# The softmax pass of a graph layer as one flat loop over a list of (super, block) steps

## The chip, the cores and the metric

The kernel runs on one core of one Trainium2 chip. The metric is the device time of one execution in microseconds (us); lower is better. The core has five engines that run side by side, each with its own queue of instructions: TensorE (PE; its weight loads are shown as PEld), VectorE (DVE), ScalarE (ACT), GpSimd (POOL) and SyncE (SP), which here only issues transfers. They are kept in step by semaphores. In a profile "PEq", "DVEq", "SPq" are the sequencers, which handle register instructions, waits and branches ahead of the engine proper.

## What is computed

One layer of a graph network with 6250 nodes and 200000 edges; the edges are sorted by the node they point to (dst). Two convolutions over the edges come first, then attention over each node's incoming edges:

```python
logits = (q[dst] * k[src]).sum(-1) * scale + (edge_attr @ ew + eb)
amax = jax.ops.segment_max(logits, dst, num_segments=n)
pe = jnp.exp(logits - amax[dst])
ssum = jax.ops.segment_sum(pe, dst, num_segments=n)
w = pe / jnp.clip(ssum[dst], 1e-06)
o = jax.ops.segment_sum(w[:, :, None] * v[src], dst, num_segments=n)
```

The change lies in the last part of it: the exponentials of the logits below their node's maximum, and the sums over each node of pe and of pe times v.

## The kernel before

The edges are cut into 392 supers of 512 edges (4 tiles of 128). The nodes are cut into 49 blocks of 128. As dst is sorted, a super touches one block, at times two or three. A word for each super in `ranges` holds its first and end block; it is read on the chip by each engine that needs it (`span`, L587: a TENSOR_LOAD and register instructions that cut the word, L597). The profile counts 440 additions at L1618, one of which is a dummy at the start, so there are 439 (super, block) pairs.

The program is a row of phases with a barrier between them: tables, conv1, node update, tables, conv2, node update, tables, `logits_pass` (logits of every edge, and maxima of windows of nodes), `node_maxima` (turns those maxima through DRAM into `max_parts`, three bf16 parts of each node's maximum), `softmax_pass`, and the last node update. The change touches `node_maxima` and `softmax_pass`.

`softmax_pass` runs a loop over supers, four slots in a turn (`slots`), and every engine has a fixed place in it. In a slot the stages belong to different supers, the lag being given by MAXIMUM, BELOW, LOAD_V, EXPONENT, WEIGHT, SCATTER = 1, 2, 2, 3, 4, 5. Inside a slot the stages that work per block run an inner loop (`pairs`) whose ends are registers:

- SP loads the 512 dst numbers of a super, spread over 128 partitions (`sm_dst`, L1508, float32), and its v rows (`sm_v`, L1513).
- ACT makes the one-hot `sm_pick` [node, edge] for each pair in two activations (L651 and L655), and the exponential (L1589).
- PE picks each edge's maximum out of `max_parts` for each pair (L684: 4 matmuls of 24 columns), between an opening and a closing matmul (L1569, L1573).
- DVE adds the three parts of the maximum (L1646), subtracts (L1648), makes the other one-hot `sm_hot` [edge, node] (L1629), and adds a pair's sums to `acc` (L1618).
- POOL multiplies v with the exponentials (L1525).
- PE sums a pair into PSUM (L1554, the scatter: 4 float32 matmuls of 136 columns, each two instructions in the trace), and then runs two matmuls of 512 columns whose result is used nowhere (FILL, L1563).

Semaphores order it: the scatter waits for `vals`, `hot` and `sums_free`, `sm_hot` for the scatter of the slot before, and SP's loads for `picked` and `vals`.

## Time and profile before

| | us |
|---|---|
| median of 3 runs | 8706.32 |
| lowest, highest | 8701.71, 8711.42 |
| the profiled execution | 8703.69 |
| its span | 8701.6 |
| mean granted TensorE clock | 0.822 of full |
| softmax pass in it, from 7201.2 to 8575.3 | 1374.1 |

The span is the time between the first and last instruction of the profiled execution; some 2 us lie around it. The phases follow one another, so a phase that becomes shorter by x us makes the execution shorter by x us, and what matters is the spacing of the pairs inside the softmax pass and the length of `node_maxima` ahead of it.

### The profile page before, as it was taken

The numbers are of one execution on the slowest core, as the hardware profiler recorded it, in microseconds if no ns is written. First come the engines' busy times: TensorE is split into PE (matmuls) and PEld (weight loads), VectorE is DVE, ScalarE is ACT, GpSimd is POOL, SyncE is SP. The second block draws the span as 40 slices with busy tenths as digits, with TensorE's granted clock in tenths as the row PEclk, the third lists the DMA queues.
The fourth block names the chain that finished last, engine by engine and source line by source line (L and its number), as shares of the span: only waits on it lengthen the run. The fifth ranks groups of instructions, "written<-read, shape, count | busy, mean of one in ns | idle before, by whom it ended". The sixth has DMA issues, their size and how long they took to land. (4 is left out here: it accounts for less than half of the span.)

```text
span 8701.6 us, 251909 instructions
## 1 busy us (share of the span) xinstructions
PE 6115.6 (70%) x44185; PEld 3967.9 (46%) x44285; DVE 5542.8 (64%) x14457; ACT 4053.9 (47%) x6964; POOL 5050.9 (58%) x5122
## 2 busy tenths in 40 slices
PE   1688888888648888888884566666655556777774
PEld 1455555555435555555553333333333324555553
DVE  4666677777666666776775566666666664444445
ACT  2445555555344555555552344444444445555552
POOL 0677777777437777777770676666655543332221
PEclk9899999999879999999996555555555559999996
DMA  4455555555225555555551666666655545554442
GB/s 144 125 135 134 134 135 134 134 136 134 66 73 134 134 134 134 134 133 133 133 131 37 173 177 173 175 173 169 159 149 145 137 110 161 161 154 148 142 138 74
DMA packets 1002317, 1182.73 MB, mean 136 GB/s; under 512 B 305441, under 2 KB 697612, under 8 KB 1000786
## 3 DMA queue, kind: packets, MB, share of 16 engines
q1 hardware_dynamic: 776470, 668.01, 27.8%
q0 software_dynamic: 225792, 514.10, 22.5%
q8 instruction: 20, 0.33, 0.0%
q14 instruction: 35, 0.29, 0.0%
HBM read 1039.63 MB, written 141.89 MB: 136 GB/s over the span
## 5 line engine op out<-in xcount | busy, mean ns | idle before, releaser
L844 POOL DMA_INDIRECT conv_rows<-src_table,conv_idx x3136 | 3114.3, 993 | 955.2 <-issue 912.9
L1265 POOL DMA_INDIRECT lg_rows<-kv_table,lg_idx x1568 | 1485.7, 948 | 958.5 <-issue 496.0
L764 PEld LDWEIGHTS ps<-conv_vals,conv_hot 128*128 128x128 f32 x7024 | 916.2, 191 | 506.2 <-issue 349.0
L1327 ACT ACTIVATE acc<-ps,neg_win 128x512 f32<-128x512 f32 x976 | 634.5, 687 | 952.7 <-DVE lg_top L1413 902.3
L947 DVE TENSOR_REDUCE conv_var<-conv_sq 128x32 f32<-128x512 f32 x784 | 536.4, 684 | 764.2 <-ACT conv_sq L908 740.6
L868 PE MATMUL ps<-conv_rows,ident_b 128*128 128x512 bf16 x2352 | 645.9, 384 | 526.9 <-DMA conv_rows<-src_table,conv_idx 480.4
L764 PE MATMUL ps<-conv_vals,conv_hot 128*128 128x129 f32 x7024 | 938.2, 276 | 109.0 <-DVE acc L750 109.0
L908 ACT ACTIVATE conv_sq<-ps 128x512 f32<-128x512 f32 x784 | 468.1, 597 | 1113.0 <-PE ps L874 997.4
L1525 POOL TENSOR_TENSOR sm_vals<-sm_v,sm_vals 128x512 f32<-128x512 f32 x392 | 414.8, 1058 | 952.9 <-ACT sm_vals L1589 952.9
L729 DVE TENSOR_TENSOR conv_hot<-conv_node_row,dst_cols 128x512 f32 (+1 forms) x878 | 604.8, 689 | 388.6 <-PE ps L764 304.3
L655 ACT ACTIVATE conv_pick<-conv_apart,one_col 128x512 f32 x878 | 633.7, 722 | 456.2 <-PE ps L684 289.2
L1554 PE MATMUL ps<-sm_vals,sm_hot 128*128 128x136 f32 x3512 | 567.8, 308 | 368.2 <-DVE acc L1618 163.0
L889 PE MATMUL ps<-conv_y,ident 128*128 128x512 f32 x1568 | 807.2, 596 | 3.5 <-DVE conv_y L977 3.5
L684 PE MATMUL ps<-dst_parts,conv_pick 128*128 x10536 | 771.0, 222 | 8.3 <-issue 4.2
L1413 DVE CUSTOM_DVE_ANT_0 acc<-ps,acc 128x512 f32<-128x512 f32 x976 | 635.4, 688 | 144.6 <-DVE tops L1368 125.1
L1288 PE MATMUL ps<-w_bias,lg_ea 39*128 39x8 bf16 x1568 | 96.0, 164 | 885.6 <-DVE logits L1394 885.6
L1554 PEld LDWEIGHTS ps<-sm_vals,sm_hot 128*128 128x128 f32 x3512 | 476.0, 204 | 423.9 <-DVE acc L1618 247.5
L684 PEld LDWEIGHTS ps<-dst_parts,lg_pick 128*128 x5268 | 524.3, 140 | 307.2 <-issue 303.9
L684 PEld LDWEIGHTS ps<-dst_parts,conv_pick 128*128 x10536 | 610.6, 99 | 116.0 <-issue 25.2
L913 ACT ACTIVATE conv_vals<-ps 128x512 f32<-128x512 f32 x784 | 468.1, 597 | 408.6 <-PE ps L889 408.5
L651 ACT ACTIVATE conv_apart<-conv_dst,neg_node 128x512 f32<-128x512 f32 x878 | 628.0, 715 | 40.1 <-DMA conv_dst<-dst_rows 20.0
L684 PE MATMUL ps<-dst_parts,lg_pick 128*128 x5268 | 634.4, 308 | 6.0 <-DVE lg_pick L669 4.9
(230 smaller groups left out, 9954.6 us busy)
## 6 DMA issues: line engine op xcount, KB each, us to landing
conv_dst<-dst_rows SPq DMA_DIRECT2D x784, 256.0 KB
v_edges<-lg_rows SPq DMA_DIRECT2D x392, 256.0 KB
sm_dst<-dst_rows SPq DMA_DIRECT2D x392, 256.0 KB, 3.3
sm_v<-v_edges SPq DMA_DIRECT2D x392, 256.0 KB, 2.7
conv_rows<-src_table,conv_idx POOLq DMA_INDIRECT x3136
lg_dst<-dst_half SPq DMA_DIRECT2D x392, 128.0 KB
conv_ea<-ea_parts SPq DMA_DIRECT2D x784, 36.0 KB
lg_rows<-kv_table,lg_idx POOLq DMA_INDIRECT x1568
```

The lines of the kernel that those rows point to most:

```text
L651: act.activation(apart, dst, ACT.Square, bias=neg_node[:, bass.ds(blk, 1)]).then_inc(picks.apart_made, 1)
L655: act.activation(picks.buffer(act, turn), apart, ACT.Relu, bias=one_col[:, 0:1], scale=-1.0).then_inc(picks.made, 1)
L684: last = pe.matmul(to[:, j, :], names, part, start=False, stop=False, skip_group_check=True)
L729: dve.tensor_tensor(hot[:, :, :], node_row[:, bass.ds(blk, 1), :].to_broadcast([P, TILES, P]), dst_cols[:, bass.ds(TILES * s, TILES)].unsq ...
L764: last = pe.matmul(bank(SUMS[g])[:, 0:self.width], self.hot[g][:, j, :], vals[:, j, 0:self.width], start=(j == 0), stop=(j == TILES - 1))
L844: pool.indirect_dma_start(rows[r][:, j, :], None, src_table, bass.IndirectOffsetOnAxis(idx[r][:, j:j + 1], 0)).then_inc(S["rows_in"][r], 16)
L868: last = pe.matmul(bank(MSG[r]).rearrange("p (j c) -> p j c", c=D), ident_b[:, :], rows[r][:, :, p * D:(p + 1) * D], start=(p == 0), stop= ...
L889: pe.matmul(bank(SHIFT[r % 2]).rearrange("p (j c) -> p j c", c=D), ident[:, :], y[r % 2][:, :, :], start=False, stop=True, skip_group_chec ...
L1265: pool.indirect_dma_start(rows[r][:, j, :], None, kv_table, bass.IndirectOffsetOnAxis(idx[r][:, j:j + 1], 0)).then_inc(S["rows_in"][r], 16)
L1327: act.activation(far[h], bank(AGAIN[r % 2]), ACT.Square, bias=neg_win[:, bass.ds(w + h, 1)], scale=PEN).then_inc(S["far"], 1)
L1413: dve.tensor_tensor_reduce(masked[h], bank(SPREAD_TO[r % 2]), far[h], 1.0, NEG, ALU.subtract, ALU.max, top[:, h:h + 1]).then_inc(S["top"], 1)
L1554: last = pe.matmul(bank(SUMS[r % 2])[:, 0:ACC_W], hot[r % 2][:, j, :], vals[r][:, j, :], start=(j == 0), stop=(j == TILES - 1))
```

## The change

`node_maxima` now also makes a list of steps. DVE takes the two block numbers of each super, makes running sums of the pair counts (9 additions over 392 numbers), PE spreads two rows over all partitions, and a loop over columns of 256 steps each finds super and block of every step. The codes are turned by PE, packed two to a word (15 bits each), written to `steps_d` in DRAM and read back into one partition of the memory that held `dst_parts`. The number of turns is `(pairs + 9) >> 2`, here (439 + 9) >> 2 = 112, so that the loop runs over 448 steps; those past the end name a spare block, number 49, that nothing reads. The maxima are stored negated.

`softmax_pass` is one loop over these steps, with no inner loop. Each of SP, PE and DVE reads one word for two steps and cuts super and block from it. The stages are:

- SP: dst (now from `dst_half`, int16, half the bytes) and v for every step, in that order, each with a wait of its own.
- DVE: the one-hot pick (L1759: compare 512 int16 numbers with the node number), `sm_hot` (L1751), and the addition (L1742). L1646 and L1648 are gone.
- PE: the scatter as before (L1686), and BELOW: one matmul of 32 columns (L1699), 16 matmuls of 8 columns (L1703: for each tile a large constant and the three negated parts), and the logits through the identity in float32 (L1706). Edges that don't belong to the step's block end at -2^64, so that their exponential is 0. The FILL matmuls and L1560 are gone.
- ACT: the exponential alone, read from PSUM (L1717).
- POOL: as before (L1667).

```diff
+STEP_BITS, SUPER_BITS = 15, 9
+STEP_COLS = 76
+STEP_WORDS = STEP_COLS * P
...
-        dst_parts = sb("dst_parts", [P, BLOCKS, 3, D], BF16)
-        acc = sb("acc", [P, BLOCKS, ACC_W])
+        dst_raw = sb("dst_raw", [P, 2 * STEP_WORDS], BF16)
+        dst_parts = dst_raw[:, 0:BLOCKS * 3 * D].rearrange("p (b k c) -> p b k c", k=3, c=D)
+        steps, turns, columns = dst_raw[0:1, :].bitcast(I32), sb("turns", [1, 1], I32), sb("columns", [1, 1], I32)
+        acc = sb("acc", [P, BLOCKS + 1, ACC_W])
...
+                        pe.wait_ge(summed, 1)
+                        pe.matmul(bank(1)[:, 0:SUPERS], ones[:, :], sums[:, TOTALS, BEHIND:BEHIND + SUPERS], start=True, stop=True)
+                        pe.matmul(bank(2)[:, 0:SUPERS + 1], ones[:, :], gaps[:, :], start=True, stop=True).then_inc(spread, 1)
+                        pe.wait_ge(coded, 1)
+                        for h in range(2):
+                            last = pe.transpose(bank(3)[0:STEP_COLS, h * P:(h + 1) * P], block_of[:, :, h], ident[:, :])
+                        last.then_inc(turned, 1)
...
+                        sp.wait_ge(packed, 1)
+                        sp.dma_start(steps_d.rearrange("(c p) -> c p", p=P), codes[:, 0, :]).then_inc(stored, 16)
+                        sp.wait_ge(stored, 16)
+                        sp.dma_start(steps, steps_d.rearrange("(a n) -> a n", a=1)).then_inc(stored, 16)
+                        sp.wait_ge(stored, 32)
...
+                        while reach < SUPERS:
+                            done(dve.tensor_tensor(sums[:, 1 - now, BEHIND:], sums[:, now, BEHIND:],
+                                                   sums[:, now, BEHIND - reach:BEHIND - reach + SUPERS], ALU.add))
+                            reach, now = 2 * reach, 1 - now
...
+                        done(dve.tensor_scalar(turns[:, :], turns[:, :], 9, None, ALU.add))
+                        done(dve.tensor_scalar(turns[:, :], turns[:, :], 2, None, ALU.arith_shift_right))
...
+                        with dve.Fori(0, last_column) as c:
+                            done = chain(dve, walk, base + COLUMN_STEPS * c)
+                            for h in range(2):
+                                at = lambda x: x[:, bass.ds(c, 1), h]
+                                done(dve.tensor_scalar(under[:, :], bank(1)[:, 0:SUPERS], at(step_f), None, ALU.is_le))
+                                done(dve.tensor_reduce(at(super_of), under[:, :], AX.X, ALU.add))
+                                done(dve.tensor_tensor(under[:, :], under[:, :], gaps_of[:, 0:SUPERS], ALU.mult))
+                                done(dve.tensor_reduce(skipped[:, :], under[:, :], AX.X, ALU.add))
+                                done(dve.tensor_tensor(at(block_of), at(block_of), skipped[:, :], ALU.add))
...
+                PICK, BELOW, HOT, EXPONENT, WEIGHT, SCATTER, ADD = 1, 2, 2, 3, 4, 5, 6
+                LEAD = 3
...
+                    for i in range(LEAD):
+                        turn(i)
+                    with eng.Fori(LEAD, end) as i:
+                        turn(i)
...
+                            t, r, k = stage(0)
+                            if r % 2 == 0:
+                                load_word(sp, "sp", words[r // 2], 2 * k + r // 2)
+                            own = sp.snap(super_at(sp, words, r))
+                            row = dst_half[bass.ds(own, 1), :].to_broadcast([P, SUPER])
+                            rows = v_edges[bass.ds(own, 1), :, :].rearrange("a p (j c) -> (a p) j c", c=D)
+                            hold(sp, made["pick"], t - (DEPTH - 1), made["sp_paced"])
+                            sp.dma_start(dst[r][:, :], row).then_inc(dst_in[r], 16)
+                            hold(sp, made["vals"], t - (DEPTH - 1), made["sp_paced"])
+                            sp.dma_start(v[r][:, :, :], rows).then_inc(v_in[r], 16)
...
-                                for _ in range(FILL):
-                                    pe.matmul(bank(SPARE), ident_b[:, :], constant[:, :], start=True, stop=True)
...
+                                t, r, k = stage(SCATTER)
+                                pe.wait_ge(made["vals"], t + 1)
+                                pe.wait_ge(made["hot"], t + 1)
+                                wait(pe, made["added"], t - 1)
+                                for j in range(TILES):
+                                    last = pe.matmul(bank(SUMS[r % 2])[:, 0:ACC_W], hot[r][:, j, :], vals[r][:, j, :],
+                                                     start=(j == 0), stop=(j == TILES - 1))
+                                last.then_inc(made["sums"], 1)
+                            if stage(BELOW):
+                                t, r, k = stage(BELOW)
+                                if r % 2 == 0:
+                                    load_word(pe, "pe", words[r // 2], 2 * k + r // 2)
+                                blk, own = block_at(pe, words, r), super_at(pe, words, r)
+                                top = max_parts[:, bass.ds(blk, 1), :, :].rearrange("p a k c -> p (a k) c")
+                                own = logits[:, bass.ds(own, 1), :].rearrange("p a c -> p (a c)")
+                                to = bank(BELOW_AT[r % 2])[:, 0:TILES * HEADS]
+                                wait(pe, made["weight"], t - 1)
+                                pe.matmul(to, digit_w[:, :], far_row[:, :], start=True, stop=False, skip_group_check=True)
+                                pe.wait_ge(made["pick"], t + 1)
+                                for j in range(TILES):
+                                    for part in [far_cols[:, :]] + [top[:, p, :] for p in range(3)]:
+                                        pe.matmul(to[:, j * HEADS:(j + 1) * HEADS], pick[r % 2][:, j * P:(j + 1) * P], part,
+                                                  start=False, stop=False, skip_group_check=True)
+                                pe.matmul(to, ident[:, :], own, start=False, stop=True, skip_group_check=True).then_inc(made["below"], 1)
...
+                                act.wait_ge(made["below"], t + 1)
+                                wait(act, made["sums"], t - (DEPTH - 1))
+                                act.activation(vals[r][:, :, D:ACC_W], bank(BELOW_AT[r % 2])[:, 0:TILES * HEADS].rearrange("p (j h) -> p j h", h=HEADS),
+                                               ACT.Exp).then_inc(made["weight"], 1)
...
+                            if stage(ADD):
+                                t, r, k = stage(ADD)
+                                to = acc[:, bass.ds(dve.snap(added_to[r], min_val=0, max_val=BLOCKS), 1), :].rearrange("p a c -> p (a c)")
+                                dve.wait_ge(made["sums"], t + 1)
+                                wait(dve, made["added"], t)
+                                dve.tensor_tensor(to, bank(SUMS[r % 2])[:, 0:ACC_W], to, ALU.add).then_inc(made["added"], 1)
+                            if stage(HOT):
+                                t, r, k = stage(HOT)
+                                blk = block_at(dve, words, r)
+                                dve.reg_mov(added_to[r], blk)
+                                own = dst_cols[:, bass.ds(TILES * super_at(dve, words, r), TILES)].unsqueeze(2).to_broadcast([P, TILES, P])
+                                start = first[:, bass.ds(blk, 1)]
+                                if not isinstance(t, int) or t >= DEPTH:
+                                    hold(dve, made["sums"], t - (DEPTH - 1), made["dve_paced"])
+                                dve.scalar_tensor_tensor(hot[r][:, :, :], own, start, lanes, ALU.subtract, ALU.is_equal).then_inc(made["hot"], 1)
+                            if stage(PICK):
+                                t, r, k = stage(PICK)
+                                if r % 2 == 0:
+                                    load_word(dve, "dve", words[r // 2], 2 * k + r // 2)
+                                nodes = node_of[:, bass.ds(block_at(dve, words, r), 1)]
+                                wait(dve, made["below"], t - 1)
+                                hold(dve, dst_in[r], 16 * (k + 1), made["dve_paced"])
+                                dve.tensor_scalar(pick[r % 2][:, :], dst[r][:, :], nodes, None, ALU.is_equal).then_inc(made["pick"], 1)
```

Two places show what stands in a row on an engine. The first is DVE in the loop of the pass, one slot of before with one pair. Names are tiles; ISA and REGISTER_ALU are register instructions of the sequencer.

```order
L1629 SCALAR_TENSOR_TENSOR sm_hot<-dst_cols,sm_first,ps 128x512
L615 ISA
L1618 ISA
L1618 TENSOR_TENSOR acc<-ps,acc 128x136
L1496 ISA
L605 COMPARE_AND_BRANCH
L587 ISA
L587 TENSOR_LOAD ranges
L597 REGISTER_ALU
L597 ISA
L597 REGISTER_ALU
L1640 ISA
```

After these come one more register instruction, L1646 and L1648. Now one step on the same engine:

```order
L1742 ISA
L1742 TENSOR_TENSOR acc<-ps,acc 128x136
L1625 ISA
L1746 REGISTER_ALU
L1746 ISA
L1751 REGISTER_ALU x2
L1751 ISA
L1751 SCALAR_TENSOR_TENSOR sm_hot<-dst_cols,sm_first,ps 128x512
L1621 TENSOR_LOAD dst_raw
L1621 ISA
L1759 REGISTER_ALU x2
L1759 ISA
```

The branches of the inner loop and the reduction with its dependent subtraction are gone, and the pick L1759 stands at the end of the step; the load of a word comes in every second step. The second place is PE. Before, behind the scatter of a slot:

```order
L1554 MATMUL ps<-sm_vals,sm_hot 128x136 x4
L1496 ISA
L605 COMPARE_AND_BRANCH
L1560 MATMUL ps<-ident_b 128x1
L1563 MATMUL ps<-sm_constant,ident_b 128x512 x2
L1569 MATMUL ps<-sm_zeros,digit_w 128x96
L605 UNCONDITIONAL_BRANCH
L605 ISA
L684 ISA
L684 MATMUL ps<-max_parts,sm_pick 128x24
```

Now:

```order
L1686 MATMUL ps<-sm_vals,sm_hot 128x136 x4
L1625 ISA
L1699 MATMUL ps<-sm_far_row,digit_w 128x32
L1703 MATMUL ps<-sm_far_cols,sm_pick 128x8
L1703 REGISTER_ALU x2
L1703 ISA
L1703 MATMUL ps<-max_parts,sm_pick 128x8
L1703 ISA
L1703 MATMUL ps<-max_parts,sm_pick 128x8
L1703 ISA
L1703 MATMUL ps<-max_parts,sm_pick 128x8
L1703 MATMUL ps<-sm_far_cols,sm_pick 128x8
```

The two wide matmuls and the branches went; 16 narrow ones came, of which the first three parts each need a register instruction of their own. In the loop of four steps the order of the changed program has, beside data instructions, 45 register and branch instructions and 2 loads on PE, 51 and 2 on DVE, 21 and 2 on SP; before it had on DVE 61 and 4 for four slots with one pair each.

## Rows read from the trace of the kernel before

**Rows 1.** by stretch: busy us (count) of five engines, PEclk, DMA share, GB/s

```profile
5000.00:6000.00 1000.00, 663.33 (x4336) 371.08 (x4334) 662.91 (x2010) 426.93 (x908) 688.08 (x727) 0.51 0.65 174
...
7202.00:7219.00 17.00, 7.68 (x36) 5.04 (x37) 11.19 (x17) 11.20 (x18) 3.74 (x4) 0.50 0.77 233
...
7400.00:8000.00 600.00, 427.93 (x3170) 302.71 (x3215) 276.97 (x742) 321.32 (x566) 187.35 (x178) 0.95 0.52 156
```

**Rows 2.** groups of the pass: count, busy us, mean ns, idle before and releasers

```profile
L1554 PE MATMUL ps<-sm_vals,sm_hot 128*128 128x136 f32 x3477 | 562.7, 309 | 366.2 <-DVE acc L1618 161.0 <-issue 114.9 <-POOL sm_vals L1525 89.4
...
L1525 POOL TENSOR_TENSOR sm_vals<-sm_v,sm_vals 128x512 f32<-128x512 f32 x390 | 412.7, 1058 | 947.3 <-ACT sm_vals L1589 947.3
L1629 DVE SCALAR_TENSOR_TENSOR sm_hot<-dst_cols,sm_first,ps 128x512 f32<-128x512 f32 x435 | 324.5, 746 | 279.6 <-PE ps L1554 183.4 <-issue 95.9
...
L1563 PE MATMUL ps<-sm_constant,ident_b 128*128 128x512 bf16 x676 | 225.9, 405 | 10.0 <-issue 3.6
```

**Rows 3.** timeline of DVE inside the pass: start, length, instruction, idle before

```profile
7753.68 0.75 DVE L1629 SCALAR_TENSOR_TENSOR sm_hot<-dst_cols,sm_first,ps 128x512 f32<-128x512 f32 x1 [2.45 <-PE ps L1554]
7754.34 0.29 DVE L1618 TENSOR_TENSOR acc<-ps,acc  x1
7755.51 0.26 DVE L1646 TENSOR_REDUCE sm_highest<-ps 128x32 f32<-128x96 f32 x1 [0.88 <-issue]
...
7756.50 0.75 DVE L1629 SCALAR_TENSOR_TENSOR sm_hot<-dst_cols,sm_first,ps 128x512 f32<-128x512 f32 x1 [0.38 <-issue]
...
7759.17 0.75 DVE L1629 SCALAR_TENSOR_TENSOR sm_hot<-dst_cols,sm_first,ps 128x512 f32<-128x512 f32 x1 [0.39 <-issue]
```

**Rows 4.** timeline of PE and its weight loads (PEld) near the pass's end

```profile
8507.71 2.17 PE L1554 MATMUL ps<-sm_vals,sm_hot 128*128 128x136 f32 x8 [0.36 <-POOL sm_vals L1525]
...
8518.40 0.17 PEld L684 LDWEIGHTS ps<-max_parts,sm_pick 128*128 x4
...
8518.76 0.47 PEld L684 LDWEIGHTS ps<-max_parts,sm_pick 128*128 x4 [0.20 <-issue]
...
8526.61 1.19 PE L1554 MATMUL ps<-sm_vals,sm_hot 128*128 128x136 f32 x8 [0.67 <-issue]
```

**Rows 5.** timeline of SP's queue (SPq): two transfers issued one behind the other

```profile
7763.40 0.33 SPq L1513 DMA_DIRECT2D sm_v<-v_edges  x1
...
7764.00 0.33 SPq L1508 DMA_DIRECT2D sm_dst<-dst_rows  x1
```

**Rows 6.** the page's DMA issues: KB each, median us from issue to landing

```profile
sm_dst<-dst_rows SPq DMA_DIRECT2D x392, 256.0 KB, 3.3
```

**Rows 7.** SP's own waits in the pass: us in total, times, longest

```profile
SPq L83 <- POOL sm_vals L1525: 568.4, 342, 5.3
```

**Rows 8.** single lines: shortest, median and longest ns

```profile
L587 DVEq TENSOR_LOAD <-ranges x342: 300/305/326, 7302.2 to 8497.0; - x171
...
L669 DVE TENSOR_SCALAR lg_pick<-lg_dst,node_of x439: 352/353/594, 4818.1 to 7151.0; 128x512 int16 x147
```

**Rows 9.** timeline: POOL's multiply and DVE's subtraction beside it, and one without

```profile
7212.52 1.06 POOL L1525 TENSOR_TENSOR sm_vals<-sm_v,sm_vals 128x512 f32<-128x512 f32 x1 [11.09 <-ACT sm_vals L1589]
...
7213.02 0.60 DVE L1648 TENSOR_TENSOR sm_below<-logits,sm_highest 128x32 f32<-128x32 f32 x1
...
7755.93 0.19 DVE L1648 TENSOR_TENSOR sm_below<-logits,sm_highest 128x32 f32<-128x32 f32 x1 [0.17 <-DVE sm_highest L1646]
```

**Rows 10.** timeline where the maxima end and the pass begins, and its last instruction

```profile
7189.47 0.33 SPq L1441 DMA_DIRECT2D max_nodes<-by_window  x1
...
7197.36 0.56 DVE L1455 CAST max_parts<-max_by_block 128x392 bf16<-128x392 f32 x1 [7.92 <-DMA max_by_block<-max_nodes]
...
7201.22 1.30 SPq L1508 DMA_DIRECT2D sm_dst<-dst_rows  x3
...
7205.06 5.61 DVE L1609 MEMSET acc<- 128x6664 f32 x1 [1.34 <-issue]
...
8575.03 0.30 DVE L1618 TENSOR_TENSOR acc<-ps,acc  x1 [1.55 <-PE ps L1554]
```

More of the change, by code:

```diff
@@ L1488, in enter @@
[L1488 to L1500 removed]
+                dst, v = deep("dst", [P, SUPER], I16), deep("v", [P, TILES, D])
```

263 lines of the change are left out of this document (131 added, 132 removed).

## The prediction

> **What bounds the kernel now.** I read the table by stretch first. The logits pass holds PE at half clock, 0.51, with PE busy 0.66; the softmax pass runs at 0.95 with PE busy 0.71, DVE 0.46, ACT 0.54, POOL 0.31 [rows 1]. No engine is full, so the spacing of the pairs must come from hand-overs and from sequencers. The groups say so: PE's scatter stood idle 366 us in the pass and `sm_hot` on DVE 280 us, mostly for each other [rows 2]. Then the seam: the pass lasts from SP's first load at 7201.22 to the end of the last addition at 8575.33, 1374.1 us [rows 10]. That is 1374.1 / 439 = 3.13 us for a pair.
>
> The timeline of DVE shows of what a pair is made. Three `sm_hot` start at 7753.68, 7756.50 and 7759.17, 2.82 and 2.67 us apart, and the last two stood idle before for "issue" alone [rows 3]. DVE's data instructions fill some 1.5 us of that. The rest is its sequencer: from the addition (7754.34) to L1646 (7755.51) are 1.17 us, in which stand one load of a word, 0.305 us [rows 8], and some ten other things (8 register or branch instructions, a wait, the dispatch). (1.17 - 0.305) / 10 = 0.087, so I take **0.09 us for a small sequencer instruction on DVE**, an estimate. Test on before: 61 / 4 = 15.3 small ones a slot, 3 waits and 4 dispatches make 22.3 x 0.09 = 2.0, plus the load 0.31, plus 0.42 for the subtraction that must wait for the end of L1646 (7755.93 - 7755.51) [rows 3, 9]: 2.7 us. The rows have 2.67 to 2.82, the mean 3.13. So before is bound by DVE's sequencer, and runs 1.15 above its own count through waits on PE.
>
> **The change part by part.** I cost one step on each engine, as all are in order and a step passes through each.
>
> DVE: 51 / 4 = 12.8 small instructions, 2 waits, 3 dispatches: 17.8 x 0.09 = 1.60, plus half a load 0.15: 1.75 us. Its data work is 0.75 + 0.29 + the pick; the same form (512 int16 numbers against a node number) took 0.353 in the logits pass [rows 3, 8]. Sum 1.39, hidden under the sequencer. L1646, L1648 and the dependent 0.42 are gone.
>
> PE: a register instruction with the narrow matmul behind it costs 0.12: four such weight loads took 0.47 where the sequencer made the pace ((0.47 - 0.10) / 3), and 0.17 where they were queued, 0.025 apart [rows 4]. 45 / 4 = 11.3 small, 2 waits: 13.3 x 0.12 = 1.60. The 14 matmuls without a register instruction between them at 0.025 are 0.35, half a load 0.15: 2.1 us; with 0.10 for a small one 1.8. I take 2.0. PE's own work at full clock is the scatter 1.19, 17 short ones x 0.025 = 0.43, two float32 loads for the identity at 1.19 / 8 = 0.15 each: 1.9, partly under the sequencer. The FILL matmuls that go (226 us busy in the records [rows 2]) ran in PE's gaps and free nothing by themselves.
>
> SP: two transfers at 0.60 from issue to issue [rows 5], half a load, 3 more small: 1.65 us. dst now stands behind v in the queue, and v waits for POOL four steps back; SP already waits 568 us so [rows 7]. From vals(n-5) to vals(n) that loop costs 0.6 + 0.35 to issue, 3.3 to land [rows 6], 0.35 pick, about 1.7 on PE and ACT, 1.06 POOL: 7.4 us for 5 steps, 1.5 a step. Hidden below 2.0. POOL needs 1.06 plus a hand-over, ACT less.
>
> So **the slowest queue needs 2.0 us** where before needed 2.7. The waits now reach 3 to 6 steps back (four `hot`, four `vals`) and no stage waits for the same step on the engine it just served; I add 0.25 for what is left, less than the 0.4 of before: T = 2.25.
>
> A small matmul costs PE 0.025 when queued [rows 4]. The Trainium skill, "TensorE: Matmul & The Clock Gate", Part 1, has that floor too, but adds that with decoding in microcode each takes about 62 ns. By the page 16 would be 1.0 us in place of 0.4 and PE some 2.6 a step; the rows speak for the smaller number.
>
> Number of steps: 448 (9 more than pairs), 9 x 2.25 = 20 us of empty work, counted in. Start of the pass: before, `acc`'s memset ran from 3.8 to 9.5 us into the pass [rows 10]; now it stands ahead of DVE's first pick, 8.5 us. The last step's scatter and addition come 3 us late. **Pass after = 11.5 + 448 T** = 11.5 + 1008 = 1019.5 us, against 1374.1.
>
> The list: no row shows it, so I build it from an instruction over 392 numbers, 0.56 [rows 10], 0.60 with its wait. Ahead of the loop 14 of these and two longer ones, 10.7; 11 short ones at 0.25 and two others, 3.9; the loop runs (439 + 264) >> 8 = 2 times with 8 long and 2 short and some 10 register waits: 13; the end 2.7. Then two transfers: up to 2.4 and 4 us, as near those of the maxima, where from issue at 7189.47 to the cast at 7197.36 two in a row took 7.9 [rows 10]. Sum 36.7, starting at 7189.5 as the copy does: 7226.2, with 1.4 for the barrier 7227.6. Before the pass began at 7201.2, so **+26; I take +28**, with the wait for PE's spread. Bounds: +20 (long ones partly cheaper) and +45 (every short one at 0.6). The old wait for the maxima, their casts and three instructions for the sign lie beside it.
>
> Sum: -1374.1 + 1019.5 + 28 = -326.6. Profiled execution 8703.7 - 326.6 = 8377.1; the median of before is 2.6 above it: **8380 us**.
>
> **The rivals.** In general the time is 8706.3 - 1374.1 + 28 + 11.5 + 448 T = 7371.7 + 448 T; without any saving 448 T would be 1334.6.
>
> 1. *DVE's pick and POOL's multiply shut each other out.* While POOL multiplied from 7212.52 to 7213.58, the subtraction on DVE ended at 7213.62 and took 0.60; elsewhere 0.19 [rows 9]. If the pick does the same, DVE's data work grows from 1.39 by up to 1.06 to 2.45, and with some wait T = 2.65: 7371.7 + 1187.2 = **8559**. For: both recur each step, and the step's order can lock them. Against: POOL is free half of the time. The Trainium skill, "SBUF — State Buffer", "Who interferes with whom", says that such a one-input compare in a two-port mode and a GpSimd instruction exclude one another for a whole instruction; it is this rival's rule.
>
> 2. *The clock stays at half.* PE enters the pass at half clock (0.50 from 7202 to 7219) [rows 1], and FILL, which kept it working between scatters, is gone. At half the scatter takes 2.17 [rows 4]; two identity loads at 2.17 / 8 are 0.54, the narrow ones 0.4, hand-over 0.2: T = 3.3, and PE is the bound: 7371.7 + 1478.4 = **8850, slower**. It decides against the change where T passes 1334.6 / 448 = 2.98. For: the logits pass stays at 0.51 though PE is busy 0.66 of it, much of that in short or low-row matmuls. Against: at T = 3.3 PE would be busy nearly always and over half of it with the full float32 scatter, denser than in the first 17 us of the pass now (7.68 of 17 us), after which the clock rose to 0.95. The same page on the clock gate holds that half clock is the default and activity lifts it.
>
> 3. *The waits vanish altogether.* T = 1.9: **8223**.
>
> 4. *Depth doesn't help*: engines stay in lock step through waits that sit in sequencers, T about 2.95: 8693.
>
> **How the numbers follow.** T from 2.05 to 2.45 (8290 to 8469): 0.50. Rival 1, up to 2.85: 0.22. Rival 3: 0.12, of which I leave out a third, below 1.92. Rival 2: 0.12. Rival 4: 0.04. Leaving out the last two and 0.04 at the fast end gives 8230 to 8650 with 0.80 in it; the list's bounds (-8, +17) lie inside. A measurement of this kernel can tell some 0.2%, 17 us, from no change. Faster: 0.50 + 0.22 + 0.12 + 0.02 = 0.86; same 0.02; slower 0.12.
>
> **What the profile would show.** The pass at about 1020 us with its hots 2.25 apart; PE's clock at 0.95 or more and PE busy over 0.8; picks at 0.35 if POOL doesn't hold them, up to 1.4 if it does; SP waiting less for POOL; some 28 us more between the two passes. Wrong would be: PEclk near 0.5 (rival 2), picks of 1 us (rival 1), DVE or PE idle on each other for 0.8 us a step (rival 4), or a list of over 45 us.

## Time and profile of the changed kernel: the result

| | median, us | runs | granted clock, mean |
|---|---|---|---|
| kernel before | 8704.15 | 4 (8701.71 to 8711.42) | |
| changed kernel | 8761.89 | 4 (8752.45 to 8765.83) | 0.751 |

The ratio is 1.0063, with a 95% interval from 1.0046 to 1.0081: the change makes the kernel 0.6% slower, where 8380 us were forecast and 8230 to 8650 was the range. The profiled execution spans 8750.2 us.

The page by forty slices (of some 219 us each, digits in tenths) says what happened. The softmax pass fills the 34th to the 39th slice and part of the two beside them:

```profile
PE   1688888888557888888884666666655549999995
...
PEclk9899999999779999999996555555555555555555
```

PE is full from there to the end of the pass, and its clock never leaves 5 tenths. In the kernel before the same stages ran at 0.95 with PE busy 0.71 [rows 1]. The table by stretch of the changed kernel (busy us and count for PE, PEld, DVE, ACT and POOL, then PEclk, DMA share, GB/s):

```profile
7215.00:7230.00 15.00, 6.65 (x70) 5.67 (x70) 11.99 (x11) 1.05 (x4) 3.17 (x3) 0.50 0.50 147
7230.00:7600.00 370.00, 369.92 (x3184) 333.50 (x3184) 238.38 (x354) 23.29 (x118) 124.59 (x118) 0.50 0.43 126
...
8000.00:8590.00 590.00, 589.85 (x5072) 531.23 (x5072) 378.90 (x564) 37.10 (x188) 197.99 (x188) 0.50 0.44 125
```

In 590 us PE is idle for 0.15 us. 188 multiplies of POOL in 590 us are 3.14 us a step. The groups of the pass, 7230 to 8600 (count, busy us, mean ns, idle before and its releaser), answer to [rows 2]:

```profile
L1686 PE MATMUL ps<-sm_vals,sm_hot 128*128 128x136 f32 x3486 | 943.3, 452 | 0.3
...
L1667 POOL TENSOR_TENSOR sm_vals<-sm_v,sm_vals 128x512 f32<-128x512 f32 x436 | 460.6, 1056 | 910.3 <-ACT sm_vals L1717 910.3
L1759 DVE TENSOR_SCALAR sm_pick<-sm_dst,node_of 128x512 bf16<-128x512 int16 x436 | 427.1, 980 | 69.3 <-issue 67.3
...
L1742 DVE TENSOR_TENSOR acc<-ps,acc 128x136 f32 x436 | 130.7, 300 | 258.7 <-PE ps L1686 258.7
...
L1717 ACT ACTIVATE sm_vals<-ps 128x32 f32<-128x32 f32 x436 | 86.0, 197 | 1284.9 <-PE ps L1706 1284.9
```

The scatter's matmul has a mean of 452 ns where before had 309, and stands idle 0.3 us in the whole pass where before had 366. So the waits that the change was to take away are indeed gone; every other engine now waits for PE. The pick on DVE takes 980 ns in the mean; [rows 8] has 353 for its form.

One step, in the timeline of the changed kernel (start, length, instruction, idle before):

```profile
8000.89 2.16 PE L1686 MATMUL ps<-sm_vals,sm_hot 128*128 128x136 f32 x8
...
8001.55 1.06 POOL L1667 TENSOR_TENSOR sm_vals<-sm_v,sm_vals 128x512 f32<-128x512 f32 x1 [2.21 <-ACT sm_vals L1717]
8001.87 0.89 DVE L1759 TENSOR_SCALAR sm_pick<-sm_dst,node_of 128x512 bf16<-128x512 int16 x1 [0.32 <-issue]
...
8002.98 0.20 PE L1699 MATMUL ps<-sm_far_row,digit_w 2*128 2x32 bf16 x1
8003.29 0.30 DVE L1742 TENSOR_TENSOR acc<-ps,acc 128x136 f32 x1 [0.54 <-PE ps L1686]
8003.56 0.61 PE L1706 MATMUL ps<-logits,ident 128*128 x2
...
8004.19 2.18 PE L1686 MATMUL ps<-sm_vals,sm_hot 128*128 128x136 f32 x8
```

PE's step is the scatter, 2.09 us to the next instruction; then the constant row and 16 narrow matmuls, 0.58 (8002.98 to 8003.56); then the identity with two float32 loads, 0.43 in three steps of four and 0.57 to 0.63 in the fourth, which is the one shown. The pick began at 8001.87, under POOL's multiply of 8001.55 to 8002.61, and ended at 8002.76, just behind it.

From SP's first `sm_dst` at 7215.03 to its last, 447 steps later, are 1398.8 us: **T = 3.13 us**, the measure by which the passes are compared below.

The seam, where the list of steps is made (answering to [rows 10]; the four transposes of the maxima stand at 7175.8 here and at 7187.5 in before):

```profile
7192.56 0.63 DVE L1541 TENSOR_SCALAR max_under<-ps,max_step_f 128x392 f32<-128x392 f32 x1 [0.61 <-DVE max_block_of L1532]
...
7204.71 0.24 DVE L1547 TENSOR_SCALAR max_super_of<-max_super_of 128x152 f32<-128x152 f32 x1 [0.21 <-DVE max_block_of L1545]
...
7207.47 0.25 SPq L1482 DMA_DIRECT2D steps_d<-max_codes  x1
...
7209.64 0.21 SPq L1484 DMA_DIRECT2D dst_raw<-steps_d  x1
...
7215.03 0.37 SPq L1650 DMA_DIRECT2D sm_dst<-dst_half  x1
```

From the transposes to the first load of the pass are 39.2 us (7215.03 - 7175.8); before, 13.7 (7201.22 - 7187.5). The list costs 25.5 us. The stages ahead of it ended 11.7 us earlier in this execution than in that of before, and the change doesn't touch those.

### The profile page after: what moved, and what is told of

Same layout as the page of the kernel before. It is cut to its first block and busy times, and to the rows that moved or that the text cites. A ratio compares the mean times of both kernels' runs of the same rounds, so it can differ in the third digit from the quotient of the medians.

```text
span 8750.2 us, 252225 instructions
## 1 busy us (share of the span) xinstructions
PE 6531.3 (75%) x49078; PEld 4528.4 (52%) x49079; DVE 5834.3 (67%) x14184; ACT 3416.9 (39%) x6139; POOL 5099.3 (58%) x5175
## 5 line engine op out<-in xcount | busy, mean ns | idle before, releaser
L1667 POOL TENSOR_TENSOR sm_vals<-sm_v,sm_vals 128x512 f32<-128x512 f32 x444 | 469.1, 1056 | 932.8 <-ACT sm_vals L1717 932.8
L1686 PE MATMUL ps<-sm_vals,sm_hot 128*128 128x136 f32 x3544 | 958.9, 452 | 0.3
L1686 PEld LDWEIGHTS ps<-sm_vals,sm_hot 128*128 128x128 f32 x3544 | 839.9, 335 | 11.5
L693 PE MATMUL ps<-dst_raw,conv_pick 128*128 x10536 | 766.1, 221 | 8.4 <-issue 3.9
L693 PEld LDWEIGHTS ps<-dst_raw,lg_pick 128*128 x5268 | 525.7, 142 | 309.2 <-issue 306.1
L693 PEld LDWEIGHTS ps<-dst_raw,conv_pick 128*128 x10536 | 606.8, 98 | 115.2 <-issue 24.4
L693 PE MATMUL ps<-dst_raw,lg_pick 128*128 x5268 | 635.7, 311 | 5.6 <-DVE lg_pick L678 4.8
```

The source lines that it names most:

```text
L693: last = pe.matmul(to[:, j, :], names, part, start=False, stop=False, skip_group_check=True)
L1686: last = pe.matmul(bank(SUMS[r % 2])[:, 0:ACC_W], hot[r][:, j, :], vals[r][:, j, :], start=(j == 0), stop=(j == TILES - 1))
```

## The experiments

Theory A: the change lost the full clock because it took FILL out. Theory B: something else in the new pass holds it down. Once that was settled, two questions followed: what bounds the pass at full clock (P: PE; V: DVE, with its pick held up by POOL), and whether the clock depends on how the pass is entered.

### FILL put back, and taken from the kernel before

```diff
 last.then_inc(made["sums"], 1)
+for _ in range(2):
+    pe.matmul(bank(5)[:, :], ident_b[:, :], constant[:, 0:512], start=True, stop=True)
```

> The changed kernel, with the two 128x512 bf16 FILL matmuls of the kernel before put back behind each step's scatter (they write a bank that nobody reads). Theory A: the change lost the full clock because it took FILL out; with FILL the pass goes back to 0.95 or more. PE then needs 1.19 for the scatter, 0.10 + 0.42 + 0.30 for the difference and 2 x 0.213 for FILL, 2.44 us a step in place of 3.14: 8762 + 448 x (2.44 - 3.14) = 8448 us, up to 8542 if VectorE's pick and GpSimd's multiply together set 2.65. Theory B: something else in the new pass holds the clock down, its fullness for one (PE busy 1.00 of the pass). The granted clock stays 0.50 and FILL costs 2 x 0.427 a step: 8762 + 448 x 0.85 = 9145 us.

Measured: 8440.58 us (8436.33 to 8446.00), ratio to before 0.9696 [0.9683, 0.9710]. Its pass:

```profile
7230.00:7260.00 30.00, 23.91 (x203) 18.48 (x203) 20.11 (x24) 1.38 (x7) 7.40 (x7) 0.51 0.46 138
7260.00:7300.00 40.00, 39.19 (x484) 30.81 (x483) 33.30 (x50) 3.35 (x17) 17.97 (x17) 1.00 0.58 160
7300.00:7600.00 300.00, 292.00 (x3625) 230.16 (x3622) 253.78 (x375) 24.64 (x125) 132.10 (x125) 1.00 0.58 164
```

The clock is at 1.00 from 7260 on and a step takes 2.42 us, 0.71 less than without 1024 columns of work that nobody needs. Theory A holds; theory B's 9145 is ruled out, since PE is busy 0.97 of the time here as well.

With one FILL matmul in place of two (`range(1)`):

> As the run with two FILL matmuls a step, but with one. Theory A, and one is enough to keep the full clock: PE 2.23 us a step, VectorE's sequencer (1.75 to 2.0) and the waits near it: 8762 + 448 x (2.25 - 3.14) = 8363 us, or near 8500 if VectorE's pick and GpSimd's multiply set 2.5. Theory A, and one is not enough: clock 0.50, T = 3.14 + 0.43 = 3.57, 8953 us. Theory B: 8953 us too, so this run tells A from B only together with the one of two.

Measured: 8953.34 us (8950.60 to 8958.80), ratio 1.0286 [1.0271, 1.0300]; the pass from 7300 to 8800:

```profile
7300.00:8800.00 1500.00, 1499.48 (x11736) 1203.55 (x11735) 902.95 (x1259) 82.62 (x419) 442.90 (x420) 0.50 0.39 110
```

The clock stayed at half, and T is 3.56: the matmul added its 0.43 to a full queue.

FILL only behind the first seven scatters, six each time:

```diff
+for _ in range(6 if isinstance(t, int) else 0):
+    pe.matmul(bank(5)[:, :], ident_b[:, :], constant[:, 0:512], start=True, stop=True)
```

> The changed kernel with six FILL matmuls behind each of the first seven scatters alone, none in the loop. Theory A1 (the clock has two stable states here: what is too thin at half clock, 3.14 us a step, is dense enough at full clock, where a step is shorter): the clock rises in the first 30 us of the pass and stays up, T near 2.2, 8762 + 20 - 448 x 0.94 = 8360 us. Theory A2 (the new loop cannot hold the full clock however it enters): the clock rises for a stretch and falls back to 0.50, 8765 to 8785 us. Theory B: never rises, 8782 us.

Measured: 8762.74 us (8750.13 to 8764.89), ratio 1.0063 [1.0049, 1.0077], theory A2. The last of these FILL matmuls starts at 7266.9, and the stretches around it are:

```profile
7248.00:7252.00 4.00, 4.00 (x52) 2.71 (x51) 2.05 (x3) 0.20 (x1) 1.06 (x1) 1.00 0.26 97
...
7272.00:7276.00 4.00, 3.95 (x56) 3.52 (x55) 2.97 (x6) 0.39 (x2) 2.11 (x2) 1.00 0.70 183
7276.00:7280.00 4.00, 3.70 (x35) 3.45 (x35) 2.81 (x6) 0.39 (x2) 2.11 (x2) 0.80 0.65 199
7280.00:7284.00 4.00, 4.00 (x47) 3.52 (x46) 2.44 (x5) 0.20 (x1) 1.06 (x1) 0.50 0.54 157
```

The clock was up before 7248 and was lost again some 11 us after the last FILL had started, in the stretch in which PE has 0.3 us without work. Lifted in this way, the new loop by itself doesn't hold it.

The kernel before without FILL:

```diff
-                FILL = 2
+                FILL = 0
```

> The kernel before with FILL = 0, nothing else. It prices that one part of the change by itself. Theory A: the pass falls to clock 0.50. Each of the 439 pairs then has 2.17 for the scatter, about 0.6 for the maximum and subtraction, and the waits between VectorE and TensorE that the old order has: T about 3.9 in place of 3.13, 8706 + 439 x 0.8 = 9057 us (bounds 8900 to 9150). Theory B, by which FILL has nothing to do with the clock: 8690 to 8706 us at 0.95.

Measured: 8756.61 us (8754.86 to 8763.76), ratio 1.0061 [1.0046, 1.0075]. The mechanism was right, the price was not:

```profile
7230.00:8600.00 1370.00, 1157.54 (x6239) 955.59 (x6237) 641.53 (x1609) 700.49 (x1229) 400.32 (x379) 0.50 0.49 145
```

The pass runs at half clock, but the old order has room: the scatter, which stood idle 366 us in the pass [rows 2], takes the longer matmuls partly into its gaps and now stands idle 210:

```profile
L1554 PE MATMUL ps<-sm_vals,sm_hot 128*128 128x136 f32 x3401 | 925.5, 453 | 210.0 <-DVE acc L1618 143.4 <-issue 42.9 <-POOL sm_vals L1525 13.7
```

The pass grows by 51 us, not by 350. The four together:

| | FILL 2 x 512 | no FILL |
|---|---|---|
| order of before | 8704 (0.95 in the pass) | 8757 (0.50) |
| new order, with its list | 8441 (1.00) | 8762 (0.50) |

Reordering with FILL in place is worth 263 us (some of it can be the clock, which rose from 0.95 to 1.00), and nothing at half clock; FILL is worth 53 us in the old order and 321 in the new one. The change made both steps at once, and each price was worked out as if the other stood still.

### What bounds the pass at full clock

The next twelve kernels ran on three other chips, four on each, on which the stages ahead of the pass take longer: the kernel before takes 11,406 us beside the first four kernels, 11,290 and 11,409 beside the others, and in the run with FILL of 2 x 384 the transposes before the list stand at 9912.7 where e1_fill2 has 7187.8. The pass itself takes what it took on the first chip where the same kernel ran on both (T = 2.21 for FILL 2 x 256 with the clock lifted, below), so it is compared by T.

GpSimd multiplies one tile of four (the values of the other three are zero):

> The changed kernel with two FILL matmuls a step, and GpSimd multiplies only the first of the four tiles of a step (the values of the other three are left at zero, so their part of the sum is missing from the result). The multiply goes from 1.06 to some 0.3 us. With FILL a step takes 2.40 us, in which VectorE's pick takes 1.06 in place of 0.35. Theory V (the pick and the multiply exclude each other, and VectorE's 0.75 + 0.29 + 1.06 with its issue sets the 2.40): the picks fall below 0.5 and T falls to TensorE's own load, about 2.3: 8441 - 448 x 0.1 = 8396 us. Theory P (TensorE's queue sets it: 0.97 busy, the rest its word loads): the picks fall as well, but T stays: 8435 to 8445 us. Theory N (no exclusion; the pick is slow by itself in this pass): the picks stay at 1.0.

Measured: 11,141.1 us; T = 2.42, no different from e1_fill2. All the picks of this run (shortest, median and longest ns):

```profile
L1765 DVE TENSOR_SCALAR sm_pick<-sm_dst,node_of x447: 346/431/519, 9951.2 to 11025.7; 128x512 bf16<-128x512 int16 x149
```

In e1_fill2 the median is 1085 ns. So GpSimd's multiply does lengthen the pick, by 0.65 us, and it costs nothing: theory P.

FILL of 384 columns in place of 512:

> The changed kernel with two FILL matmuls a step of 384 columns in place of 512. At full clock that takes 2 x 0.053 = 0.11 off TensorE's 2.40 to 2.44 us a step. Theory P (TensorE sets T): 8441 - 448 x 0.11 = 8392 us. Theory V (VectorE sets T): 8441 us. If the full clock does not hold with so little work: 0.50 and T = 3.14 + 2 x 0.32 = 3.78, 9048 us.

Measured: 11,103.7 us, T = 2.30 (1028.2 / 447), clock 1.00: 0.12 us a step, where P had 0.11 and V nothing. Its pass on PE alone, where one turn of the loop (four steps) ends:

```profile
10502.35 1.17 PE L1687 MATMUL ps<-sm_vals,sm_hot 128*128 128x136 f32 x8
...
10504.53 1.17 PE L1687 MATMUL ps<-sm_vals,sm_hot 128*128 128x136 f32 x8
...
10507.13 1.19 PE L1687 MATMUL ps<-sm_vals,sm_hot 128*128 128x136 f32 x8 [0.25 <-issue]
```

Three steps of four take 2.18 to 2.19 us, and PE's instructions follow each other without a gap; the fourth takes 2.60.

The pick made by ScalarE, in two instructions:

```diff
-dve.tensor_scalar(pick[r % 2][:, :], dst[r][:, :], nodes, None, ALU.is_equal)
+act.activation(apart[r % 2][:, :], dst[r][:, :], ACT.Square, bias=neg_nodes)
+act.activation(pick[r % 2][:, :], apart[r % 2][:, :], ACT.Relu, bias=one_col, scale=-1.0)
```

> The changed kernel with two FILL matmuls a step, and ScalarE makes the one-hot of the nodes (Square of the difference, then Relu of one minus it, 0.72 us each as in the kernel before) in place of VectorE. ScalarE then has 1.44 + 0.20 and its sequencer, some 2.1 us a step, VectorE only 1.04 and its sequencer. Theory P: T stays 2.40, 8441 us. Theory V: T falls to TensorE's load, 2.3, 8396 us. ScalarE as a new bound (in-order exponent behind two activations): T up to 2.6, 8530 us.

Measured: 11,138.3 us, T = 2.42: P again.

The pick as a two-input instruction of VectorE (`scalar_tensor_tensor(pick, dst, nodes, ones, is_equal, mult)`):

> The changed kernel with two FILL matmuls a step, and VectorE makes the pick with a two-input instruction (compared with the node number, times a tile of ones), which computes the same. Theory V: a two-input instruction does not exclude GpSimd's multiply; it takes 0.55 to 0.75 us in every step in place of 1.06, and T falls by 0.1, 8396 us. Theory P: the duration falls, T stays at 2.40, 8441 us. Theory N: it is no shorter than 1.06.

Measured: 11,148.5 us, T = 2.41. The expectation of 0.55 to 0.75 us was wrong; the group from 10100 to 10900:

```profile
L1763 DVE SCALAR_TENSOR_TENSOR sm_pick<-sm_dst,node_of,sm_constant 128x512 bf16<-128x512 int16 x334 | 473.5, 1418 | 37.7 <-issue 35.9
```

It takes 1.42 us, and T is what it was. The first two picks of the pass, made before POOL's first multiply, took 0.75 and 0.74 us and the third, under it, 1.50; so this form is held up as well. VectorE had just room for it: it is busy 754.75 of the 800 us.

TensorE's load of a word of the list moved from behind FILL into the scatter, with FILL 2 x 384:

```diff
 for j in range(TILES):
     last = pe.matmul(...)
+    if j == 1 and stage(BELOW)[1] % 2 == 0:
+        word_of(stage(BELOW))
```

> The changed kernel with two FILL matmuls of 384 columns, and TensorE's load of a word of the list stands between the second and third matmul of the scatter in place of behind FILL. With FILL of 384 columns a step takes 2.30 us, of which TensorE stands idle for issue 0.32 + 0.25 us in two steps, behind the load. Theory P (TensorE's queue sets T): the load is covered by matmuls already queued, T = 2.30 - 0.2 = 2.1, 90 us off the pass (1028 to 940). Theory V (VectorE, whose pick is held to the end of GpSimd's multiply, is near its bound with 0.88 of its time busy): T stays at 2.2 to 2.3, 0 to 40 us. The clock stays at 1.00 in both.

Measured: 10,984.2 us beside 11,289.6, T = 2.33. No gain, rather 0.03 lost: a turn still has its step of 2.60, and one of the other three now takes 2.31 in place of 2.19. My reading of the gaps was wrong: they don't stand behind a load of a word (two in a turn) but once in a turn of the loop. With ScalarE's pick on top of it:

> As the run with the word's load in the scatter and FILL of 384 columns, and ScalarE makes the pick in two instructions of 0.72 us. It tells whether VectorE's pick holds that run. Theory V: with the pick gone from VectorE, T falls below that run's, to 2.1. Theory P: no faster than that run. If ScalarE (1.64 us busy a step and its own load and registers) becomes the bound, slower than that run: T 2.3 to 2.4.

Measured: 10,996.0 us, T = 2.33. VectorE was not what held it.

A prefetch hint for the branch at the end of TensorE's loop (`hint_back_edge`), with FILL 2 x 384, and beside it the same kernel without the hint:

> The changed kernel with two FILL matmuls of 384 columns and a branch prefetch hint at the top of TensorE's loop. With 2 x 384, three steps of four take 2.18 us and the one that closes the loop's iteration 2.63: a gap of 0.4 before the scatter. If the gap is the loop's branch fetching its instructions, the hint takes it away: T = 2.19, 112 x 0.4 = 45 us less, some 8345 us where the kernel with 2 x 384 has 8390. If VectorE, whose own loop closes as well, holds it: no change. If it is the load of the word: no change.

> The kernel with two FILL matmuls of 384 columns again, beside the other runs on one chip, and to see whether its clock rises in every run. By the spacing in its first profile 52 us less than with 512 columns: 8390 us where the kernel before has 8704.

Measured: 11,122.6 us with the hint (T = 2.34), 11,126.4 without (T = 2.31). The hint takes nothing away; the gap before the scatter at a turn's end is `[0.38 <-issue]` with it, where e6_fill2x384 has 0.25, so it costs some 0.1 us a turn. What the 0.4 us are stays open: that they come once in a turn is shown, that it is the branch is not. The clock was at 1.00 from some 35 us into the pass to its end in both profiles, and no run of either stood apart.

### How the pass is entered

FILL 2 x 320:

> The changed kernel with two FILL matmuls of 320 columns, load of the word where the changed kernel has it. 2 x 384 columns a step held the full clock, one of 512 did not. If 2 x 320 hold it: T = 2.30 - 0.053 = 2.25, 24 us less in the pass than with 384, 1004 us. If not: clock 0.50 for at least part of the pass, T = 3.14 + 0.53 = 3.67 there, up to 1640 us for the pass.

Measured: one run at 10,972.9 us, three from 11,140.8 to 11,193.8. The profile shows why:

```profile
9850.00:10300.00 450.00, 449.83 (x3556) 369.34 (x3555) 263.12 (x368) 24.12 (x122) 129.05 (x122) 0.50 0.36 107
10320.00:11000.00 680.00, 660.66 (x8809) 558.95 (x8807) 570.14 (x911) 59.92 (x303) 320.84 (x304) 1.00 0.65 176
```

The same loop ran at half clock for over 450 us, 3.69 us a step (122 in 450), then at full clock to its end, 2.24 us a step (304 in 680). Both are what its work amounts to at that level. A run at 3.69 us a step from start to end would take near 11,600 us, an estimate from 2 x 256, below, with 11,539 at 3.55. So by their times the clock rose in mid-pass in the other two of these three runs too, and near the start in the run of 10,972.9. Nothing in the program changes at 10,300; what made the clock rise there is open.

FILL 2 x 256, with the word's load moved:

> As the run with the word's load in the scatter, with two FILL matmuls of 256 columns. As many columns as the one of 512, which left the clock at 0.50; but the steps are some 0.2 us shorter at full clock. If the clock goes by work in a stretch of time once it is up but must first rise at half clock, it stays at 0.50: T = 3.57, pass about 1590 us. If the way it is cut or the shorter step lifts it: T near 2.0 to 2.2, 900 to 980 us.

Measured: 11,539.3 us, ratio 1.0222, clock 0.50 throughout, T = 3.55. The moved load alone doesn't keep the clock down: in e9_early_384, with 2 x 384, it was up 25 us into the pass. That asked for the opposite test, to lift the clock first and then give less:

```diff
+lead = isinstance(t, int)
+for _ in range(6 if lead else 2):
+    cols = SUPER if lead else 256
+    pe.matmul(bank(5)[:, 0:cols], ident_b[:, :], constant[:, 0:cols], start=True, stop=True)
```

> The changed kernel with six FILL matmuls of 512 columns behind each of the first seven scatters (they lifted the clock to 1.00 from 7246 on when they stood alone) and two of 256 columns in the loop. In the loop alone 2 x 256 left the clock at 0.50 through the whole pass. Two states with memory (what holds the full clock is less than what brings it): the clock stays at 1.00, T = 2.30 - 2 x 0.053 = 2.19, pass about 1000 us with the slow start. No memory: it falls back within some 20 us of the loop's start as it did without FILL, T = 3.57, pass about 1590 us.

Measured: 11,056.2 us beside 11,409.3, ratio 0.9694 [0.9680, 0.9709], T = 2.21:

```profile
9900.00:9950.00 50.00, 36.11 (x400) 27.61 (x404) 33.32 (x48) 3.92 (x15) 13.91 (x14) 0.79 0.42 128
...
10300.00:10600.00 300.00, 290.96 (x3973) 252.31 (x3972) 248.44 (x411) 27.00 (x137) 144.82 (x137) 1.00 0.65 179
```

The loop that stayed at half clock when it was entered at half clock (e12_early_256, apart from the moved load) stays at full clock when it is entered at full clock. With the hint and 2 x 320 in the loop:

> The changed kernel with the hint, six FILL matmuls of 512 columns behind each of the first seven scatters and two of 320 in the loop. With 2 x 320 and no lift the pass ran at 0.50 for its first 480 us and then at 1.00 to its end, and other runs of it never rose. Two states with memory: lifted at the start, it stays at 1.00: 24 us less than the kernel with the hint and 2 x 384, about 10 us more at the start. Otherwise it falls to 0.50 as before, above 8550 us.

Measured: 11,082.7 us, T = 2.29, and no run at half clock: from 11,077.4 to 11,114.8. The expectation has it that the other runs of e10_fill2x320 never rose; by their times they did, only late. The last two kernels ran on a chip like the first one. With 2 x 128 in the loop:

> As the run that lifts the clock with six FILL matmuls of 512 columns behind each of the first seven scatters, with two of 128 columns a step in the loop in place of 256. Lifted and with 2 x 256 the clock stayed at 1.00 and a step took 2.19; lifted and with nothing it fell back. If 2 x 128 hold it: T = 2.19 - 0.107 = 2.08 by TensorE, or 2.15 if VectorE now sets it (0.83 busy at 2.19): 940 to 970 us for the pass in place of 987. If not: clock 0.50 and T = 3.14 + 0.21 = 3.35, pass about 1500 us.

Measured: six runs, of 8312.3, 8393.3, 8397.3, 8491.8, 8585.4 (the profiled one) and 8756.8 us. In the profile the clock went in mid-pass, with no change of the program:

```profile
7300.00:7690.00 390.00, 377.86 (x5425) 345.13 (x5424) 316.37 (x561) 36.87 (x187) 197.53 (x188) 1.00 0.66 189
7710.00:8440.00 730.00, 730.00 (x6303) 657.02 (x6302) 463.45 (x653) 42.83 (x217) 229.83 (x218) 0.50 0.42 117
```

188 steps in 390 us are 2.07 a step, the shortest of this study; 218 in 730 are 3.35. And 2 x 256 again:

> The kernel that lifts the clock with six FILL matmuls of 512 columns behind each of the first seven scatters and has two of 256 in the loop, again, beside the kernel before in more rounds: the pass should take 987 us in place of the 1374 of before. On a chip where the kernel before takes 8704 us that gives 8704 - 387 + 25 for the list and the later start = 8342 us, ratio 0.958; on a chip where it takes 11400, 11400 - 362 = 11040, ratio 0.968. If the clock does not hold in some of the runs, they stand some 500 us higher.

Measured: **8349.32 us (8346.60 to 8356.66) beside 8705.75, ratio 0.9590 [0.9577, 0.9602]**, T = 2.21. This version beats both kernels, and its runs lie within 10 us of each other. PE at a turn's end and behind it:

```profile
7800.38 0.39 PE L1711 MATMUL ps<-logits,ident 128*128 x2
7801.01 1.19 PE L1687 MATMUL ps<-sm_vals,sm_hot 128*128 128x136 f32 x8 [0.25 <-issue]
...
7804.12 0.38 PE L1693 MATMUL ps<-sm_constant,ident_b 128*128 128x256 bf16 x2
7804.43 0.18 PE L1704 MATMUL ps<-sm_far_row,digit_w 2*128 2x32 bf16 x1
7804.97 0.39 PE L1711 MATMUL ps<-logits,ident 128*128 x2
7805.19 1.17 PE L1687 MATMUL ps<-sm_vals,sm_hot 128*128 128x136 f32 x8
```

A step is 1.01 us of scatter (to the FILL behind it), 0.31 of FILL, 0.54 for the constant row and 16 narrow matmuls, 0.22 for the identity: 2.08. Once in four steps 0.41 more: 0.63 from the identity to the scatter at 7801.01, in place of 0.22.

## Why the prediction was wrong, point by point

**The step that failed** is that the FILL matmuls "ran in PE's gaps and free nothing by themselves". That they free nothing is right. That they do nothing is not: they are what held the clock at 0.95, in the old order already (0.50 in e4_before_no_fill) and in the new one (e1_fill2 against the changed kernel, 321 us). Everything that the prediction worked out for PE, 1.9 us of work and 2.0 for its queue, was for full clock, and the sum took that clock as given; only the rival asked what keeps it. So the term T was put at 2.25 and measured 3.13, which is 0.88 x 448 = 394 us; the time missed the forecast by 382.

**Rival 2 was the case, and its chance of 0.12 was too small.** Its mechanism, place and sign were right: PE the bound, clock 0.50, slower beyond a T of 2.98. It was given 8850 us; at the measured T of 3.13 the prediction's own formula gives 7371.7 + 448 x 3.13 = 8774, and 8762 was measured. The terms of its T: scatter 2.17 taken, 2.09 to 2.11 measured; narrow matmuls 0.4 and a hand-over 0.2, together 0.58 measured; identity 0.54 taken, 0.43 measured, 0.57 to 0.63 once a turn. What spoke against it in the text was an inference: at T = 3.3 PE would be denser than in the 17 us after which the clock rose in before. The first part came true (PE busy 1.00), the conclusion did not. How dense the first 17 us were [rows 1] was not what counted, as the trace of before shows in the next stretch and in two instructions around its start:

```profile
7219.00:7240.00 21.00, 15.92 (x127) 11.20 (x129) 10.48 (x31) 12.70 (x23) 7.90 (x8) 1.00 0.67 202
...
7216.29 2.18 PE L1554 MATMUL ps<-sm_vals,sm_hot 128*128 128x136 f32 x8 [1.08 <-POOL sm_vals L1525]
...
7218.72 0.61 PE L1563 MATMUL ps<-sm_constant,ident_b 128*128 128x512 bf16 x1 [0.24 <-issue]
```

The clock rose behind one scatter and the first FILL matmul of the pass. Without FILL, and otherwise with the same program, the old pass stayed at 0.50 from its start to its end (e4_before_no_fill). What in FILL lifts the clock no run shows. The row that should have counted more stood in the same group: the logits pass, at 0.51 with PE busy 0.66 [rows 1], "much of that in short or low-row matmuls", as the prediction itself said.

The Trainium skill, "TensorE: Matmul & The Clock Gate", Part 1, has half clock as the default and a busy PE as what lifts it. The trace disagrees if busy is read as the profile's busy time: 0.50 at a busy share of 1.00 for 590 us in one stretch, and 1.00 at a share of 0.97 in e1_fill2. That the same loop can run at either level for hundreds of us is what the runs with 2 x 320 and 2 x 128 show within one execution; that the way it is entered decides is shown for 2 x 256, with the moved load as the other difference between the two kernels.

**Rival 1**, pick and multiply excluding each other: the mechanism is real (431 ns in the median with a quarter of the multiply, 1085 with all of it), its price is zero here. A multiply of a quarter and a pick on ScalarE left T at 2.42, and a pick of 1.42 us left it at 2.41, since PE was the bound. The prediction's 2.65 put the held pick on the critical path; DVE's 1.06 + 0.75 + 0.29 = 2.1 with some issue fits below 2.4. The Trainium skill, "SBUF — State Buffer", "Who interferes with whom", has the exclusion for two-port modes, and contention with a GpSimd instruction that reads SBUF for instructions with two inputs from there. The trace agrees for both forms of the pick: 0.35 us at its shortest and 1.085 in the median for the first, 0.74 and 1.42 for the second.

**T at full clock.** 2.25 was forecast without FILL. e3_fill_lead ran that loop at full clock for one turn, behind its last FILL; its scatters start here:

```profile
7268.14 1.19 PE L1687 MATMUL ps<-sm_vals,sm_hot 128*128 128x136 f32 x8
...
7270.18 1.17 PE L1687 MATMUL ps<-sm_vals,sm_hot 128*128 128x136 f32 x8
...
7272.04 1.17 PE L1687 MATMUL ps<-sm_vals,sm_hot 128*128 128x136 f32 x8
...
7273.92 1.17 PE L1687 MATMUL ps<-sm_vals,sm_hot 128*128 128x136 f32 x8
...
7276.30 1.19 PE L1687 MATMUL ps<-sm_vals,sm_hot 128*128 128x136 f32 x8 [0.35 <-issue]
```

Four steps in 8.16 us are T = 2.04; it is one turn, near the start of the pass, and no more. The loops that stood longer at full clock had 2.07 with 2 x 128 and 2.21 with 2 x 256. Taking FILL's 0.31 from the 2.08 of the latter and adding the 0.41 / 4 of the turn gives 1.87, an estimate of PE's own need. So the prediction's 1.9 for PE's work was right, and its 0.35 on top for register instructions and waits was some 0.2 too much. DVE's sequencer was no bound at 2.07 either, as the 1.75 us worked out for it allow.

**The narrow matmuls.** 0.025 us each were taken. From the constant row to the identity are 0.58 us at half clock and 0.54 at full, for 17 of them: some 0.03 each, at either clock. The number was right. The 62 ns which the Trainium skill, "TensorE: Matmul & The Clock Gate", Part 1, has for decoding in microcode don't show in any of these runs.

**The list**: +28 forecast, 25.5 measured, inside the bounds of 20 and 45. Its loop took 11.9 us (7192.56 to the end of its last instruction at 7204.50) for 13.

**The waits**: right. Scatter's idle time went from 366 us to 0.3; they were simply replaced by matmuls of twice the length. Where the clock was there, the order was worth 263 us, so rival 4 is out.

**SP and the loads**: over the whole pass SP waited 658 us for POOL in the changed kernel and 640 in before (the 568 of [rows 7] are for a shorter stretch). The forecast had it waiting less. In the changed pass it cost nothing, as PE had no gap there.

With the clock held, the forecast of 8380 stands beside 8349 for e18_lift_256_b. That they are so near is luck in part: that kernel has 0.31 us of FILL in a step which the forecast did not have, and the forecast had some 0.2 a step too much. At T = 2.04, which no run held for longer than a turn, its formula would give 7371.7 + 448 x 2.04 = 8286, so the sum by itself was some 90 us too high. What turned the saving into a loss was its condition, the clock.

## What to carry to other kernels

When a change takes out or makes denser anything on TensorE, ask first what holds the granted clock, and cost both levels, because a pass that is bound by TensorE at half clock gives back the whole gain of a better order. Busy share is no proxy for that: look for a stretch of the same kernel with the same mix of matmuls and read its clock, and test a loop both entered at half clock and entered at full clock. Useless matmuls can earn their time, and their price is read at the clock which they bring: here 2 x 256 columns a step cost 0.31 us, and with them in the loop and the clock lifted ahead of it the step went from 3.13 to 2.21.

## What the runs showed of the hardware that was not expected

- PE busy for 589.85 of 590 us at a granted clock of 0.50, in a stream with 8 float32 pieces of 136 columns and 19 short matmuls a step.
- The same loop at either level: 3.69 and 2.24 us a step in one execution with 2 x 320, 2.07 and 3.35 in one with 2 x 128; the clock rose in mid-loop in the first and fell in mid-loop in the second.
- The narrow matmuls take the same time at both clocks: 0.58 and 0.54 us for seventeen.
- Some 0.4 us on PE once in a turn of its loop (four steps) at full clock, 0.15 to 0.2 at half clock, which neither an earlier load of the word nor a branch hint took away.
- A two-input compare from int16 and bf16 takes 1.42 us beside GpSimd's multiply and 0.74 without it; the one-input form takes 1.06 and 0.35.
